# A kernel of two attentions and two feed-forward blocks: the second head's f16 exponentials converted on VectorE instead of computed a second time on ScalarE

## The reference, cut to what matters

```python
s = jnp.einsum('bhid,bhjd->bhij', q, k) * SCALE
p = jax.nn.softmax(s, axis=-1)
o = jnp.einsum('bhij,bhjd->bhid', p, v)
```

## Times and profile of the kernel before

| what | value |
|---|---|
| time, median of 3 runs | 1096.37 us (1090.71 to 1099.45) |
| time of the profiled execution | 1091.27 us |
| its span in the profile | 1089.5 us |
| PE busy | 903.8 us (83%) |
| DVE busy | 779.3 us (72%) |
| ACT busy | 726.2 us (67%) |
| POOL busy | 622.3 us (57%) |
| steps of the first attention, about | 58 to 504 us |
| steps of the second attention, about | 758 to 972 us |

### The profile page before, as it was taken

The page is one execution under the profiler, slowest core; times in us unless marked ns, Lnnn a source line. Parts: engine busy times, 40 slices in busy tenths (PEclk is TensorE's granted clock), DMA queues, the critical chain, the costliest instruction groups (busy, mean ns, idle before and its releaser), DMA issues. The chain is left out here.

```text
span 1089.5 us, 23585 instructions
## 1 busy us (share of the span) xinstructions
PE 903.8 (83%) x8849; PEld 689.9 (63%) x8854; DVE 779.3 (72%) x1550; ACT 726.2 (67%) x1222; POOL 622.3 (57%) x571
## 2 busy tenths in 40 slices
PE   4887999999999999997546999968888989973486
PEld 4655686767776777675435999956566767663143
DVE  5768778778877887676785444438888786747796
ACT  3387978788878888884442444435697878952674
POOL 2177766766686667673425555442686867853142
PEclk9899999999999999998867999989799999986698
DMA  9579999899989998996741222253999989983155
GB/s 262 172 129 186 162 151 157 143 187 149 172 149 172 158 156 137 158 172 100 240 150 56 76 74 78 69 191 114 175 167 201 155 157 150 182 136 116 27 118 126
DMA packets 455248, 158.80 MB, mean 146 GB/s; under 512 B 428097, under 2 KB 445697, under 8 KB 455105
## 3 DMA queue, kind: packets, MB, share of 16 engines
q1 hardware_dynamic: 451392, 147.06, 70.5%
q0 software_dynamic: 3744, 10.23, 3.0%
HBM read 38.62 MB, written 12.71 MB: 47 GB/s over the span
## 5 line engine op out<-in xcount | busy, mean ns | idle before, releaser
L477 POOL TENSOR_TENSOR A_PHL<-A_pr,A_PHL 128x508 f16<-128x508 f32 x256 | 294.9, 1159 | 133.5 <-ACT A_pr L754 132.6
L753 ACT ACTIVATE A_PHL<-A_ps,A_negmax 128x508 f16<-128x508 f32 x256 | 179.2, 700 | 17.5 <-DVE A_negmax L1003 14.8
L477 POOL TENSOR_TENSOR C_PHL<-C_pr,C_PHL 128x512 f16<-128x512 f32 x128 | 150.2, 1183 | 55.9 <-ACT C_pr L754 55.3
L754 ACT ACTIVATE A_pr<-A_ps,A_negmax 128x508 f32<-128x508 f32 x256 | 181.1, 707 | 0.0
L1003 DVE TENSOR_REDUCE A_negmax<-A_ps 128x2 f32<-128x1016 f32 x128 | 154.2, 1205 | 0.0
L598 PE MATMUL A_ps<-A_K,A_Q 64*128 64x512 f32 x768 | 123.7, 427 | 12.4 <-ACT A_pr L754 9.7
L616 PE MATMUL A_ps<-A_VH,A_PT 128*128 128x65 bf16 (+1 forms) x1024 | 109.5, 197 | 18.7 <-DMA A_PT<-A_PHL 18.4
L616 PEld LDWEIGHTS A_ps<-A_VH,A_PT 128*128 128x128 f16 (+1 forms) x1024 | 93.6, 98 | 47.3 <-DMA A_PT<-A_PHL 29.8
L617 PE MATMUL A_ps<-A_VL,A_PT 128*128 128x64 f16 (+1 forms) x1024 | 108.5, 194 | 0.0
L618 PE MATMUL A_ps<-A_VH,A_PT 128*128 128x65 bf16 (+1 forms) x1024 | 108.3, 195 | 0.0
L753 ACT ACTIVATE C_PHL<-C_ps,C_negmax 128x512 f16<-128x512 f32 x128 | 88.7, 693 | 15.9 <-DVE C_negmax L1003 15.2
(11 more groups left out here) (349 smaller groups left out, 2653.2 us busy)
## 6 DMA issues: line engine op xcount, KB each, us to landing
A_PT<-A_PHL SPq DMA_TRANSPOSE x256, 3.4
M_WINl<-in_L_ffn_w_in SPq DMA_DIRECT2D x4, 1024.0 KB, 11.8
M_WOUTl<-in_L_ffn_w_out SPq DMA_DIRECT2D x4, 1024.0 KB, 12.6
C_yc<-routed_rows SPq DMA_DIRECT2D x8, 512.0 KB, 5.5
ct_split<-A_CT SPq DMA_DIRECT2D x4, 768.0 KB, 4.2
C_CT<-ct_split SPq DMA_DIRECT2D x4, 768.0 KB, 7.8
M_rows<-M_xn SPq DMA_DIRECT2D x4, 512.0 KB, 9.0
out<-X SPq DMA_DIRECT2D x16, 128.0 KB, 2.0
```

The source lines that it names most:

```text
L477: pool.tensor_tensor(PHL[:, e % PRING, 1, 0:KEYS], pr[:, e % RING, 0:KEYS], PHL[:, e % PRING, 0, 0:KEYS], ALU.subtract).then_inc(pl_ready. ...
L753: a.activation(PHL[:, e % PRING, 0, 0:KEYS], o, ACT.Exp, bias=nm[:, n % 4, h:h + 1])
L754: a.activation(pr[:, e % RING, 0:KEYS], o, ACT.Exp, bias=nm[:, n % 4, h:h + 1]).then_inc(p_ready.sem, 1)
```

## The change

It makes the f16 exponentials of the second head (h = 1) of each step by a conversion of the f32 ones. Of ACT's four exponentials per step three are left. DVE gets an operation per step, `cast(n)`, which stands after the maxima of step n + 1 and waits for the f32 exponentials of both heads of step n. POOL's second subtraction of a step now waits for that conversion (`p_cast`) instead of `p_ready`. The ring of `pr`, the transposing DMAs and PE's order stay.

```diff
                 for h in range(2):
                     e = 2 * n + h
-                    wait(pool, p_ready, e + 1)
+                    if h == 0:
+                        wait(pool, p_ready, e + 1)
+                    else:
+                        wait(pool, p_cast, n + 1)
                     pool.tensor_tensor(PHL[:, e % PRING, 1, 0:KEYS], pr[:, e % RING, 0:KEYS], PHL[:, e % PRING, 0, 0:KEYS],
...
                     if e >= RING:
                         wait(a, pl_ready, e - RING + 1)
-                    a.activation(PHL[:, e % PRING, 0, 0:KEYS], o, ACT.Exp, bias=nm[:, n % 4, h:h + 1])
+                    if h == 0:
+                        a.activation(PHL[:, e % PRING, 0, 0:KEYS], o, ACT.Exp, bias=nm[:, n % 4, h:h + 1])
                     a.activation(pr[:, e % RING, 0:KEYS], o, ACT.Exp, bias=nm[:, n % 4, h:h + 1]).then_inc(p_ready.sem, 1)
...
+            def cast(n):
+                e = 2 * n + 1
+                wait(v, p_ready, e + 1)
+                v.tensor_copy(PHL[:, e % PRING, 0, 0:KEYS], pr[:, e % RING, 0:KEYS]).then_inc(p_cast.sem, 1)
...
                     v.tensor_reduce(nm[:, g % 4, :], ps[:, S_BANK + 2 * (g % 2):S_BANK + 2 * (g % 2) + 2, 0:KEYS], AX.X,
                                     ALU.max, negate=True).then_inc(max_ready.sem, 1)
+                if 1 <= g <= G:
+                    cast(g - 1)
+                if g < G:
                     nb = g // U + 1
```

More of the change, by code:

```diff
@@ L309, in attention @@
         p_ready = sem("p_ready", 2 * G)
+        p_cast = sem("p_cast", G)
         pl_ready = sem("pl_ready", 2 * G)
```

## The result

| what | before | changed |
|---|---|---|
| time, median | 1096.28 us (1090.71 to 1099.45, 4 runs) | 1122.74 us (1116.01 to 1128.05, 4 runs) |
| ratio of changed to before | | 1.024, 95% interval 1.019 to 1.029 |
| profiled execution, its span | 1091.27, 1089.5 us | 1126.29, 1124.5 us |
| PE busy | 903.8 us | 921.0 us |
| DVE busy | 779.3 us | 865.6 us |

The kernel became 2.4% slower, 26 us by the medians, where 3.5 us had been forecast. The work moved as foreseen (ACT -103 us, DVE +86 us); what it does to PE was sized wrongly.

A forecast was written before the change was run, and what follows sets the result against it. PE was taken to bound the first attention, DVE being fullest early in the second. The terms -5 + 3 - 1.5 + 2 + 4 + 1 gave +3.5 us on 1096.37, stated as 1099 us; range 1080 to 1116, the forecast's own 1091 to 1107.

The forecast's parts named there:

- hidden: First attention's steady part: 47 us of conversions fit beside 89 idle us of DVE, so they cost nothing.
- ACT's relief: One of ACT's four exponentials fewer per step shortens PE's waits on ACT in the first attention: -5 us, bound -6.7.
- almost all could go, 5.6 us: First attention's steady part: PE's 12 waits on ACT, 0.53 us on average, could nearly all vanish.
- Conversion 0.43 us: Each of 192 conversions on DVE takes 0.43 us, 82 us of DVE in all.
- Light steps: Second attention's light steps: pairs of steps get slower through the chain of DVE and POOL, +3 us, ends -7 and +5.5.
- The chain of 2.92 us a step: Two POOL subtractions, the conversion between them and two handovers follow one another, taking 2.92 us a step.
- The three waits for K: Second attention: PE's three waits of about 4 us for K's low part shrink, -1.5 us, ends -3 and +2.
- The full DVE at the start: First 82 us of the second attention: DVE has 9.5 us free, conversions bring 10.8; +2 us, ends 0 and +6.
- Later transposes: Head 1's later subtraction delays the transposes, lengthening 19 waits of PE by 0.2 us each: +4 us, ends 0 and +10.
- Ends: After each attention's last step nothing hides the conversion; each ends some 0.4 us later: +1 us.
- Rival 1: The exclusion between DVE and POOL becomes the bound, 2.92 us wherever PE's step is shorter: +20, 1116 us; chance 0.18.
- light pairs at 5.6 to 5.8 us: Sign in the second attention: scores two light steps apart take 5.6 to 5.8 us where they took 5.47.

The follow-up runs named there:

- number 1: The changed kernel without the conversion; POOL's second subtraction waits for ACT alone and head 1's f16 part is zero: 1089.6 us, 0.995 of the kernel before.
- number 3: The changed kernel with a 256-element reduction on DVE in place of the conversion, same place and waits: 1110.3 us, 1.015 of the kernel before.
- number 11: The kernel before, with the statistics of the second attention's later two batches moved to each batch's first steps: 1090.7 us, 0.997 of the kernel before.
- Number 10: The changed kernel with the conversion written as a reduction, one element at a time, same values: 1126.9 us, 1.031 of the kernel before.
- number 2: The changed kernel, but POOL's second subtraction does not wait for the conversion and uses head 0's f16 exponentials: 1119.8 us, 1.023 of the kernel before.

## Why the prediction was wrong

The step that failed is the price of the conversions in DVE's queue. The prediction put it at nothing in the first attention ("hidden"), at -1.5 us for the waits for K and at +2 us for the full DVE at the start of the second. Against number 1, which has the relief and no conversion, they cost 11.9 us in the first attention and 17.2 us in the second. Term by term:

- **ACT's relief (-5, and up to -7 in the second attention's light steps): too large.** The -5 stood for the first attention alone, where number 1 measures -1.9 us; in the second it measures -4.2. That the whole gain is about 5 us agrees with the -5 by chance. The step "almost all could go, 5.6 us" took a wait's length for its worth. In the first attention the next wait in PE's order, the transposes, took 6.3 of 6.8 us back.
- **Conversion 0.43 us: right undisturbed** (medians 0.42 and 0.45), and 74.0 + 41.2 = 115 us instead of 82 with what they sit out. The text saw the exclusion in the earlier trace rows and put it into a chain for the light steps alone. The 1.12 us in the earlier trace rows belong to a `TENSOR_TENSOR`, not to a conversion; that conversions are held too shows in their own range, 0.41 to 2.0 us.
- **Light steps (+3): wrong sign.** The scores of light steps late in the second attention of the changed kernel:

```profile
957.45 0.96 PE L602 MATMUL C_ps<-C_K,C_Q 64*128 64x512 f32 x6
...
962.25 0.96 PE L602 MATMUL C_ps<-C_K,C_Q 64*128 64x512 f32 x6
...
967.37 0.96 PE L602 MATMUL C_ps<-C_K,C_Q 64*128 64x512 f32 x6
```

  Two steps take 4.80 and 5.12 us. The same steps took 5.40 and 5.71 us before and take 4.80 and 5.11 us in number 1; 5.6 to 5.8 were forecast. The 18 steps of the second attention that took less than 2.92 us before are together 6.0 us shorter now, and 7.6 us in number 1, so here most of the relief arrives. The term was 9 us too high, and what the heavy steps cost is larger than the miss of the total shows. The chain of 2.92 us a step does not bite. That the ring and the lag carry POOL over the light steps is the likely reason, and was not tested.
- **The three waits for K (-1.5): wrong sign, and the largest miss in the second attention.** Measured +11.2 us of waiting (12.1 to 23.3), and 17.1 - 10.2 = 6.9 us more of lowered clock in C. Of this waiting 2.0 us are there in number 1. The three old waits grew to 5.17, 5.89 and 6.34 us, and three new ones of 3.19, 2.20 and 0.50 us stand at other heavy steps of the first two batches. The text counted one conversion in front of the chain and one subtraction fewer. It did not count that the maxima and two steps' conversions share the queue, or, which is the smaller part, that a conversion releases POOL for two subtractions just when DVE issues its tiny operations.
- **The full DVE at the start (+2, end +6): far too small.** DVE had 9.5 us free in 82 and needed 10.8 plus what is sat out. It now shows 77.6 of 82, 95%. ACT's waits for maxima grew, as the prediction said, but the relief alone does about half of that in the second attention and most of it in the first, since an ACT with less to do waits longer. In the changed kernel, in number 1 and in the kernel before (which has 14.8 us in A):

```profile
ACT C_PHL L758 <- DVE C_negmax L1013: 48.5, 34, 5.0
...
ACT A_PHL L758 <- DVE A_negmax L1013: 33.7, 27, 3.6
```

```profile
ACT C_PHL L761 <- DVE C_negmax L1016: 32.4, 28, 5.2
ACT A_PHL L761 <- DVE A_negmax L1016: 30.8, 29, 3.8
```

```profile
ACT C_PHL L753 <- DVE C_negmax L1003: 15.2, 8, 4.3
```

  So 16 us of the growth in C, and 3 us in A, go with the conversions.

- **The first attention's conversions "hidden" beside 89 idle us of DVE: wrong.** They cost 11.9 us there (number 1's 439.6 to 451.5). This is the largest term that was put at nothing. DVE's idle time is a mean over steps; in steps with several jobs there can be none. The timeline of such a step in the changed kernel:

```profile
299.58 0.77 DVE L912 CAST A_PHL<-A_pr 128x508 f16<-128x508 f32 x1
...
301.79 1.11 DVE L876 CAST A_K<-A_KI 128x8 fp32r<-128x8 f32 x1
```

  The conversion sits out a subtraction and so does the 8-element cast behind it. DVE has no gap from 298.46 to 306.15, PE stops twice (0.59 and 0.97 us), and the granted clock is 0.50 from 304.0 to 307.0: the matmuls of `weigh` take 0.24 to 0.28 us there instead of 0.20.
- **Later transposes (+4): the number came (+5.0 us), the cause did not.** Number 1 has the same waits without any conversion (23.0 us), and number 3, which keeps head 1's subtraction as late, is only 2.9 us over it in A.
- **Ends (+1): cannot be told.** The stretch between the loops is 4.3 us longer and that behind them 1.0, and without any conversion number 11 has 261.9 us between the loops and number 1 has 266.5, against 260.9 before.
- **Rivals.** Rival 1 named the side (1116 us), but its mechanism, a bound of 2.92 us in light steps, is not what happened: in the second attention those steps became shorter, and in the first the 39 steps below 2.92 us are 3.2 us longer in sum, where rival 1 had +8, with as many of them below 2.92 us as before. The rival that was missing is "DVE's queue in the heavy steps". Of the signs that were named, ACT busy near 618 us (623.0), DVE near 861 us (865.6), waits on `A_pr` below 4 us (3.8) and waits for `A_PT` above 20 us (21.7) came true, and none of them tells the forecast from what happened; the two that would have, light pairs at 5.6 to 5.8 us and three waits for K near 3.3 us, did not.
- **The clock** stood in the earlier trace rows (six scores in 1.65 instead of 0.96 us after the 3.92 us wait) and was in no term. Against number 1, (1 - granted clock) x length is 5.5 + 5.1 us more in the two loops, and PE is busy 5.7 + 4.4 us longer.
- **The sum** is 1099.9 us and not 1099, which changes nothing.

What stays open: how much of the conversion's cost is DVE sitting out POOL and how much POOL sitting out the conversion. Number 10 takes both away, but is longer itself. Why each of the other steps of the first attention loses or gains was not gone through. Nor was the place found of the 2 to 10 us by which the medians stand higher than the loops account for.

## What to carry to other kernels

Price work that is moved to another engine by the steps in which that engine is full and has the bounding engine's next input in its queue, not by its idle time over the stage. A wait that is taken away is worth its length only if the next wait in that engine's order does not grow: look for it by an experiment that only takes away. And where two engines sit out each other's operations, as DVE and POOL do here, a wait of one for the other synchronises them, so that a small operation behind it can cost a whole operation of the neighbour (0.16 us became 1.0 to 1.1).

## What the hardware showed

- A wait of PE can cost more than its length: with the one of 5.2 us went nearly 7 us at half the granted clock, with the one of 3.9 us about 3.4. In both loops 7.4 of 23.0 us were PE being busy longer with the same matmuls.
- On DVE, `TENSOR_SCALAR` and two-input operations on 128 x 4 elements in SBUF last up to 1.15 us beside a subtraction on POOL and 0.16 us without it, the reductions of numbers 3 and 10 (0.41 and 0.67 us) were not disturbed in 192 steps each, and a conversion takes 0.41 to 2.0 us. The Trainium skill ("SBUF — State Buffer", Who interferes with whom) has `tensor_scalar` and `cast`, in their two-port modes, and operations with two SBUF inputs contend with GpSimd, and reductions not; the trace agrees.
- Conversions that POOL waits for were disturbed less (median 0.42 us in A) than those that nobody on POOL waits for (0.77 us, number 2).
